# Five score slots in the last ALiBi group, its maxima earlier, and later casts of built queries and keys

## What is computed

```python
qkv = jnp.clip(x @ w_qkv.T, -8, 8); q, k, v = jnp.split(qkv, 3, axis=-1)
q, k = _layer_norm(q, q_ln_w, q_ln_b), _layer_norm(k, k_ln_w, k_ln_b)
scores = jnp.einsum('bqhd,bkhd->bhqk', q, k) * scale + slopes[:, None, None] * rel
probs = softmax(where(causal, scores, -inf))
attn = jnp.einsum('bhqk,bkhd->bqhd', probs, v)
out = attn @ w_out.T
```

## Time and profile before

| | us |
|---|---|
| median of three runs | 1548.15 |
| lowest, highest | 1544.55, 1549.65 |
| the profiled execution | 1549.18 |
| its span | 1547.3 |
| TensorE busy in the span | 1451.9 (94%) |
| VectorE, ScalarE, GpSimd busy | 905.1, 807.5, 533.6 |
| granted TensorE clock, mean | 0.975 of 2.4 GHz |
| the ALiBi stage | from 904.7 to 1268 |

### The profile page before, as it was taken

One profiled execution on the slowest core, in us unless ns is written; L12 is line 12 of the kernel. 1 busy time (PEld: TensorE's weight loads), 2 busy tenths in 40 slices (PEclk: granted clock), 3 DMA queues, 4 the chain that ended last, 5 costly groups with the idle time before them and its releaser, 6 DMA issues. The chain is left out here.

```text
span 1547.3 us, 23953 instructions
## 1 busy us (share of the span) xinstructions
PE 1451.9 (94%) x8301; PEld 1021.0 (66%) x8301; DVE 905.1 (58%) x1361; ACT 807.5 (52%) x1731; POOL 533.6 (34%) x495
## 2 busy tenths in 40 slices
PE   5799999999999999999978987999999999999996
PEld 4566776766776776677646864555555548888885
DVE  4345554545554455555567637766666417877877
ACT  3555665555665655566443422556556565433433
POOL 0234444333444333444034134313131013444442
PEclk9799999999999999999989998999999999999999
DMA  5255445344445435434510045443435114000000
GB/s 184 67 44 39 48 50 45 39 49 38 40 47 52 35 47 43 37 47 41 86 55 1 1 55 69 57 55 51 59 45 100 46 43 189 1 1 0 1 28 28
DMA packets 46785, 75.90 MB, mean 49 GB/s; under 512 B 17664, under 2 KB 23296, under 8 KB 45824
## 3 DMA queue, kind: packets, MB, share of 16 engines
q1 hardware_dynamic: 42368, 64.54, 29.2%
q0 software_dynamic: 4352, 10.49, 5.0%
HBM read 42.49 MB, written 2.10 MB: 29 GB/s over the span
## 5 line engine op out<-in xcount | busy, mean ns | idle before, releaser
L737 DVE TENSOR_REDUCE nmax<-sc 128x1 f32<-128x128 f32 (+7 forms) x256 | 192.6, 753 | 150.8 <-PE sc L482 150.8
L1610 ACT ACTIVATE l_probs<-l_banks 128x512 f32<-128x512 f32 (+3 forms) x384 | 171.8, 493 | 134.9 <-PE l_banks L1554 84.3
L1650 DVE TENSOR_REDUCE pm<-l_sm 128x2 f32<-128x1024 f32 (+1 forms) x192 | 179.2, 957 | 102.1 <-PE l_sm L1529 63.8
L665 ACT COPY pt<-tb 128x512 f32<-128x512 f32 (+3 forms) x256 | 129.3, 505 | 198.5 <-PE tb L496 195.4
L657 ACT ACTIVATE probs<-sc,nmax 128x128 f32<-128x128 f32 (+7 forms) x256 | 190.6, 745 | 54.7 <-DVE nmax L737 54.5
L496 PE MATMUL tb<-ident,probs 128*128 128x128 f32 x1152 | 174.1, 276 | 2.8 <-DVE pt L745 1.2
L78 PE MATMUL sc<-k_h,q_h 128*128 128x512 f32 (+4 forms) x384 | 144.8, 377 | 14.4 <-DVE q_l L761 8.4
L1551 PE MATMUL l_banks<-qk_bufs 128*128 128x512 f32 (+3 forms) x384 | 143.9, 417 | 6.7 <-DMA qk_bufs<-mT 3.8
L78 PE MATMUL sc<-k_l,q_h 128*128 128x512 f32 (+4 forms) x384 | 132.0, 344 | 0.0
L78 PE MATMUL sc<-k_h,q_l 128*128 128x512 f32 (+4 forms) x384 | 131.9, 344 | 0.0
L520 PE MATMUL mb<-pt,ckv 128*64 128x512 f32 (+2 forms) x736 | 131.7, 493 | 0.0
(11 more groups left out here) (282 smaller groups left out, 3109.4 us busy)
## 6 DMA issues: line engine op xcount, KB each, us to landing
gated_late<-in_gated SPq DMA_DIRECT2D x11, 768.0 KB, 14.2
wout<-in_w_out SPq DMA_DIRECT2D x16, 512.0 KB, 7.2
late<-late SPq DMA_DIRECT2D x128, 64.0 KB, 2.0
rb<-rT SPq DMA_DIRECT2D x62, 128.0 KB, 8.8
qk_bufs<-late SPq DMA_DIRECT2D x96, 64.0 KB, 6.1
qk_bufs<-late POOLq DMA_DIRECT2D x96, 64.0 KB, 6.6
nope_t<-in_nope_by_dim SPq DMA_DIRECT2D x16, 192.0 KB, 5.6
late<-in_gated SPq DMA_DIRECT2D x3, 768.0 KB, 9.2
```

The source lines that it names most:

```text
L665: act.copy(pt[i // 4][:, e, j0:j0 + nb, (i % 4) * P:(i % 4 + 1) * P], tb[TB[g]][:, 0:nb, :]).then_inc(pt_act, 1)
L737: dve.tensor_reduce(nmax[:, n % 4:n % 4 + 1], row, axes, ALU.max, negate=True).then_inc(negmax, 1)
L1610: act.activation(probs[(NC * g + c) % RING][:, h, 0:w], banks[:, (E_STEPS * g + n) % SLOTS, 0:w], ACT.Exp).then_inc(exped, 1)
L1650: dve.tensor_reduce(pm[g % 2][:, :, s, i, half], slot(("m", g, n))[:, :, 0:w], AX.X, ALU.max, negate=True).then_inc(freed, 1)
```

## The change

- **Order.** The cast of ScalarE becomes an item of its own, `("cast", chunk, which)`. In groups 0, 2 and 4 the list `ahead` has it three places behind its build; for chunk 0 both casts stand at the start, as before.
- **Maxima of the last group.** In group 6 (`g == GROUPS - 2`) `total` is smaller by four banks (2048 of 18432 columns), so that all of `ahead` is placed by 16384 columns.
- **Slots of the last group.** In group 7 the score products use five slots: the three of `banks` and the two banks of the `sm` tile that `("rows", 7, 1)` used. Item n waits for the exponential five items before it; items 3 and 4 wait for the copy to `mT`.

```diff
+    order = [("build", 0, 0), ("build", 0, 1), ("cast", 0, 0), ("cast", 0, 1)] + [("v", k, j) for j in range(6) for k in range(DK)]
...
             ahead[2:2] = [("build", g // 2 + 1, 0)]
-            ahead[5:5] = [("build", g // 2 + 1, 1)]
+            ahead[5:5] = [("cast", g // 2 + 1, 0), ("build", g // 2 + 1, 1)]
+            ahead[9:9] = [("cast", g // 2 + 1, 1)]
         first = C_HALF if g == 0 else 0
         done, total = 0, sum(chunk_cols(c)[1] * HG for c in range(first, NC))
+        if g == GROUPS - 2:
+            total -= 4 * BANK
...
+        LAST_SLOTS = SLOTS + 2
+        def e_slots(g):
+            return LAST_SLOTS if g == GROUPS - 1 else SLOTS
+        def e_slot(g, n):
+            at = n % e_slots(g)
+            return banks[:, at, :] if at < SLOTS else slot(("rows", g, 1))[:, at - SLOTS, :]
...
-                    from_one(pe, exped, E_STEPS * g + n + 1 - SLOTS)
+                    if n >= e_slots(g):
+                        pe.wait_ge(exped, E_STEPS * g + n + 1 - e_slots(g))
+                    elif n >= SLOTS:
+                        pe.wait_ge(freed, uses["rows", g, 1] + 1)
+                    else:
+                        from_one(pe, exped, E_STEPS * g + n + 1 - SLOTS)
...
-                def build(chunk, which):
+                def cast(chunk, which):
                     act.wait_ge(freed, uses["build", chunk, which] + 1)
                     act.copy(stages[2 * which].bitcast(F32R), stages[2 * which + 1]).then_inc(high, 1)
...
-                    if kind == "build":
-                        build(g, n)
+                    if kind == "cast":
+                        cast(g, n)
```

More of the change, by code:

```diff
@@ L1328, in alibi_order @@
 def alibi_order():
-    order = [("build", 0, 0), ("build", 0, 1)] + [("v", k, j) for j in range(6) for k in range(DK)]
+    order = [("build", 0, 0), ("build", 0, 1), ("cast", 0, 0), ("cast", 0, 1)] + [("v", k, j) for j in range(6) for k in range(DK)]
     late_v = [("v", k, j) for j in (6, 7) for k in range(DK)]
@@ L1542, in e @@
                     q0, w = chunk_cols(c)
-                    b, at = g % BUFS, (E_STEPS * g + n) % SLOTS
+                    b, dst = g % BUFS, e_slot(g, n)
                     if g == 0 and n == 0:
@@ L1548, in e @@
                         pe.wait_ge(rows_in, ROWS * (g + 1))
-                    from_one(pe, exped, E_STEPS * g + n + 1 - SLOTS)
+                    if n >= e_slots(g):
[4 more added lines that the diff above has]
+                        from_one(pe, exped, E_STEPS * g + n + 1 - SLOTS)
                     diagonal = q0 == j * P
-                    last = pe.matmul(banks[:, at, 0:w], keys(b, h)[:, j * P:(j + 1) * P], query_cols(b, h // 2, q0, w),
+                    last = pe.matmul(dst[:, 0:w], keys(b, h)[:, j * P:(j + 1) * P], query_cols(b, h // 2, q0, w),
                                      start=True, stop=not diagonal)
                     if diagonal:
-                        last = pe.matmul(banks[:, at, 0:P], keep.ident_b[:], keep.mask_t[:], start=False, stop=True)
+                        last = pe.matmul(dst[:, 0:P], keep.ident_b[:], keep.mask_t[:], start=False, stop=True)
                     last.then_inc(sE, 1)
@@ L1609, in exp @@
                     w = chunk_cols(c)[1]
-                    act.activation(probs[(NC * g + c) % RING][:, h, 0:w], banks[:, (E_STEPS * g + n) % SLOTS, 0:w],
+                    act.activation(probs[(NC * g + c) % RING][:, h, 0:w], e_slot(g, n)[:, 0:w],
                                    ACT.Exp).then_inc(exped, 1)
```

## The result

The changed kernel takes 1540.53 us (median of five runs, 1540.07 to 1541.21) against 1548.9 us before (median of five, 1544.55 to 1550.22). The ratio is 0.995, with a 95% interval of 0.9939 to 0.9961. In a second series it took 1540.39 against 1549.64, a ratio of 0.9933 (0.9919 to 0.9946). Both times lie in the stated range of 1534.0 to 1544.0; the gain is 8.4 and 9.2 us, where 10.2 were forecast.

The account below looks back on a forecast made before the run. TensorE, busy 94%, was taken as the bound, so only its waits or low clock could be won. Terms -2.8 + 0.4 - 2.7 - 2.9 - 2.4 + 0.2 = -10.2 from 1548.15 gave 1538.0 us, range 1534.0 to 1544.0.

Parts of the forecast that it names:

- Maxima earlier: Before group 7: TensorE's wait for `mT` goes, -2.8 us; denser work at the end of group 6 costs +0.4.
- nothing to spare: Start of group 7: copy near 1227.0 plus 5.47 us puts the first product at 1232.5, just when TensorE is ready.
- Clock: Start of group 7: the 1.2 GHz stretch behind the wait for `mT` goes with that wait, -2.7 us.
- Five slots: Group 7: each chunk's fourth score product no longer waits for an exponential, -2.9 us.
- The rival in which the pass waits in the slots' place: Group 7: the pass with the values takes over the wait, slots give nothing; 1540.9 us, chance 0.10.
- Casts: Groups 2 and 4: waits for exponentials go as casts come when their input is ready, -1.2 us each.
- +0.2: Group 0: maxima run behind VectorE, one more behind the second build; a loss of 0.2 us, between -2.1 and +1.0.
- Keys late: Rival: TensorE waits for keys' DMAs at the first maxima product of groups 2, 4, 6; 1556.7 us, chance 0.06.

Follow-up runs that it names:

- m2: Changed kernel with group 7's maxima spread over 17408 instead of 16384 columns of group 6; 1535.73 us in a single execution.
- u2: Changed kernel with group 7's maxima spread over all of group 6 again; 1542.76 us, ratio to before 0.9966.
- o2: Kernel before with the earlier maxima of group 7 alone; 1542.51 us, ratio to before 0.9969.
- o1: Kernel before with the five slots in group 7 alone; 1542.5 us, ratio to before 0.9974.
- u3: Changed kernel with each cast straight behind its build again in ScalarE's order; 1542.5 us, ratio to before 0.9959.
- b1: Changed kernel with ScalarE's two copies of a finished half in group 7 ahead of the fifth product's exponential; 1538.67 us in a single execution.
- s4: Changed kernel with four score slots in group 7 instead of five; 1537.03 us in a single execution.
- o3: Kernel before with the moved casts alone; 1545.14 us, ratio to before 0.9977.

## Why the prediction was right, and where not

- **Maxima earlier, -2.8 + 0.4: held.** Group 6 went from 37.93 to 35.70, -2.2: the wait of 2.80 went, and the group's own work grew by 0.6, not 0.4. The margin was wrong: "nothing to spare" took the 5.47 us from the copy to the product as fixed, but there were 5.56 without a wait, of which 1.0 was spare. That hid a better setting (m2).
- **Clock, -2.7: held for the profiled execution.** u2 gives 2.63 and o2 2.49. As a cost of the median run it may be too large: in the one execution profiled, o1 shows the same wait with 1.1. Also, the changed kernel has a stretch at the lower clock, of 3.4 us, at the start of the gated stage, where the kernel before had none:

```profile
1260.40:1263.80 3.40, 3.40 (x18) 3.40 (x17) 2.37 (x5) 2.77 (x6) 3.05 (x3) 0.50 0.76 139
```

  It makes the rest 0.6 longer (282.61 against 282.02). It does not follow from the shorter group 7 alone: u3 and m2 have the same group 7 and no such stretch, u2 has one behind a long group 7. But both profiled executions of the changed kernel have it, and that of the kernel before has not, so whether it comes with the kernel or with the execution is open. It was not in the sum.
- **Five slots, -2.9: mis-sized; 2.28.** The missing step is what ScalarE is late with next. I priced its exponentials, and left out its copy of the finished half, which stands behind the exponentials that have piled up once TensorE may run ahead, and for which the next pass with the values waits (1.03 and 0.34 us). The savings at the products were even larger than priced, 3.4, since the narrow chunks give as much as the others with a mask; the two passes take 1.1 back. The rival in which the pass waits in the slots' place had this mechanism for every chunk; it holds behind two of the twelve. With the copy moved (b1), slots and copy together give 2.28 + 0.84 = 3.1. The reason for the slots was right, but one of the two does nothing (s4). The twelve waits of rows 3 are not one for each chunk, as I read them: all lie in chunks 4 to 11, at first, third and fourth products, and they gave only a bound.
- **Casts, -1.2 each: held,** at -1.20 and -1.18. For group 0 I took +0.2, and it was -0.4 in its second half: the loss that I expected there did not come, and why it gained was not looked into.
- **Keys late: far off.** They went out from 1056.6 to 1061.9 and landed within 2.9, by 1064.8, 4.6 us before their use at 1069.38, where I had left 1.0. The cast and with it the issues came 4.2 us later, not 5.1. The line on landing in rows 10 is of all 24 DMAs that the view holds, SyncE's twelve for the queries with them: the 6.3 that I took for the keys was one of SyncE's, and the keys themselves took 2.8 to 5.5 us, the last landing at 1063.1. The view of line 1463 (1449 before), from 1050 to 1068, which again holds DMAs of both engines, and TensorE's row:

```profile
L1463 POOL DMA_DIRECT2D qk_bufs<-late x12: 484/492/523, 1056.6 to 1061.9; - x12
...
DMA to landing us min/median/max: 2.3/2.6/2.9
...
1069.38 0.48 PE L1539 MATMUL l_sm<-qk_bufs 128*128 128x512 f32 x1
```

  Before, part of SyncE's twelve for the queries was in flight at the same time, and the keys' median was 4.2; now the casts are 7.7 us apart instead of 4.8, the last query has landed by 1058.2, and the keys take 2.6 to 2.9. In all ten traces with the casts moved they take at most 3.1 us, in the four without (before, u3, o1, o2) up to 4.9 to 5.7. The Trainium skill (DMA: Bandwidth & Descriptors, anatomy of one DMA) would have 2.2 us for each, an estimate from its fixed cost: the trace after shows 0.4 to 0.7 more, and the trace before disagrees, with up to 5.5.

The parts measured add up: group 0 0.4, groups 2 and 4 2.4, group 6 2.2, group 7 4.7, together 9.7, less 0.6 for the rest. This is the 9.1 between the two spans, since the first half of group 0 (0.7 less) and the start (0.6 more), both at mixed clocks, cancel.

The sum had 10.2. It comes that close in part by luck: group 7 gave 0.9 less than its two terms, group 6 gave 0.2 less, and the rest cost 0.6 that was not in the sum; group 0 gave 0.6 more than its term.

## What to carry to other kernels

When an engine is let run ahead by more slots, list every item of the engine that empties them, not only the ones that free the slots: the next wait is for the item that stands behind the backlog. Give as many slots as remove the wait and no more; try the next smaller number. A margin for a DMA that is read from one place holds for what was in flight there: move the work and the margin moves too, in both directions.

## What was not expected of the hardware

- The same idle time of TensorE (2.54 and 2.56 us) was followed by 6.8 us at 1.2 GHz in one execution and 3.4 in another, which is 2.6 or 1.1 us of time. Behind the waits of 2.80 (before) and 2.53 us (o3) it was 6.8.
- The start of the gated stage, the same in all kernels and behind the same two idle times of TensorE (0.80 and 1.45 us), had a stretch of 3.4 us at 1.2 GHz in some profiled executions (changed kernel twice, u2, s4) and none in the others: 0.6 to 0.7 us.
- Four DMAs of 8 KB took 3.8 to 4.1 us from the first issue to the end of the last packet in the four traces where an instruction packet fell among them, and 3.25 us in the ten where it did not.
